# Regrouping the cross-attention rounds of a decoder layer by the shape in which TensorE's array is used

## The reference

```python
q = (layer_norm(latents) @ Wq)   # 16 heads of 64
k, v = split(layer_norm(context) @ Wkv)
k = apply_rope(k, cos, sin)
attn = softmax(clip(q k^T * 64**-0.5, -11, 11))
out = (attn v) @ Wo + bo         # added to x
```

## Time and profile before

| | |
|---|---|
| time, median of 3 runs | 442.52 us (440.68 to 444.0) |
| the profiled execution's own time | 440.72 us |
| its span, first to last instruction | 438.6 us |
| PE busy, share of the span | 413.8 us, 94% |
| PE weight loads | 306.8 us, 70% |
| DVE, POOL, ACT busy | 323.6, 258.2, 194.7 us |
| first scores of round 0, of round 30 | 60.83, 283.40 us |

### The profile page before, as it was taken

How to read it: one execution, slowest core, us unless ns; L and a number is a source line. 1 busy time by engine, 2 the same in 40 slices (tenths; PEclk the granted TensorE clock), 3 DMA queues, 4 the chain that set the end, 5 groups by cost and what they waited for, 6 DMA issues and landing times.

```text
span 438.6 us, 8443 instructions
## 1 busy us (share of the span) xinstructions
PE 413.8 (94%) x3157; PEld 306.8 (70%) x3157; DVE 323.6 (74%) x686; ACT 194.7 (44%) x310; POOL 258.2 (59%) x228
## 2 busy tenths in 40 slices
PE   3997899999999999999999999999998999999996
PEld 2666666766667766667775676768876788888884
DVE  8798758978778857986776798798676972755554
ACT  6758463746364435463544644443547453000000
POOL 6847438998778878797779674686634581000000
PEclk9999999999999999999999999999999999999999
DMA  7676405000000000000000000335627670000000
GB/s 182 175 174 93 87 11 94 0 1 0 1 2 0 1 2 0 1 1 0 2 2 0 2 1 0 147 55 81 145 36 201 116 140 1 6 6 13 6 6 13
DMA packets 75433, 19.83 MB, mean 45 GB/s; under 512 B 66741, under 2 KB 73834, under 8 KB 75394
## 3 DMA queue, kind: packets, MB, share of 16 engines
q1 hardware_dynamic: 72628, 18.27, 19.7%
q10 hardware_dynamic: 2766, 1.04, 1.0%
HBM read 17.27 MB, written 2.02 MB: 44 GB/s over the span
## 4 chain that ended last, share of the span: by engine, by line
PE 71%; DVE 12%; issue 6%; ACT 4%; POOL 3%; DMA 2%; ACTq 1%; DVEq 0%; POOLq 0%
PE psum L1191 11%; PE psum L1174 11%; PE psum L984 9%; PE psum L1365 5%; PE psum L1366 5%; PE psum L1367 5%; PE psum L1210 3%; PE psum L1332 3%; PE psum L1334 3%; PE psum L1333 3%; PE psum L1201 3%; PE psum L1093 3%; POOL xeT_lo L583 2%; DVE rden L1591 1%; ACT e_sb L811 1%
## 5 line engine op out<-in xcount | busy, mean ns | idle before, releaser
L543 POOL TENSOR_TENSOR e_part<-e_sb 128x512 f32<-128x512 f32 x64 | 89.0, 1409 | 29.7 <-DVE e_sb L1584 29.7
L811 ACT ACTIVATE e_sb<-psum 128x1024 f32<-128x1024 f32 x64 | 62.2, 1022 | 16.2 <-PE psum L1174 16.2
L1174 PE MATMUL psum<-q_t,kT 64*128 64x256 f32 x512 | 64.2, 390 | 0.0
L1191 PE MATMUL psum<-e_sb,v_sb 128*64 128x256 f32 x512 | 63.4, 386 | 0.0
L1791 DVE SCALAR_TENSOR_TENSOR x_sb<-psum,dw,x_sb 128x128 f32<-128x128 f32 x96 | 33.7, 351 | 35.8 <-PE psum L1367 33.2
L1591 DVE RECIPROCAL rden<-psum 128x256 f32<-128x256 f32 x32 | 55.8, 1745 | 0.2 <-PE psum L1201 0.2
L790 ACT ACTIVATE kT<-psum 128x512 f32<-128x512 f32 x32 | 19.1, 597 | 78.2 <-PE psum L1093 77.9
L1174 PEld LDWEIGHTS psum<-q_t,kT 64*128 64x128 f32 x512 | 46.8, 187 | 9.5 <-issue 5.0
L1584 DVE TENSOR_SCALAR e_sb<-e_sb 128x1024 f32<-128x1024 f32 x64 | 50.5, 824 | 3.8 <-ACT e_sb L811 3.8
L535 POOL TENSOR_TENSOR k_rot<-rope_a,rope_b 128x512 f32<-128x512 f32 x32 | 41.8, 1309 | 12.8 <-DVE rope_b L1471 12.8
L1191 PEld LDWEIGHTS psum<-e_sb,v_sb 128*64 128x64 f32 x512 | 33.5, 136 | 21.5 <-issue 5.8
(11 more groups left out here) (193 smaller groups left out, 764.9 us busy)
## 6 DMA issues: line engine op xcount, KB each, us to landing
w_raw<-in_L_ffn_W_dram SPq DMA_DIRECT2D x96, 64.0 KB, 2.3
gates<-gate_dram SPq DMA_DIRECT2D x6, 768.0 KB, 4.4
ctx_sb<-in_ctx_dram SPq DMA_DIRECT2D x4, 256.0 KB, 6.0
vbd<-v_dram SPq DMA_DIRECT2D x16, 52.6 KB
v_dram<-v_tok SPq DMA_DIRECT2D x4, 136.0 KB, 3.0
raw<-in_L_xattn_Wkv_dram SPq DMA_DIRECT2D x2, 256.0 KB, 5.1
k_rot<-in_L_xattn_Wkv_dram SPq DMA_DIRECT2D x2, 256.0 KB, 4.5
k_rot<-in_L_xattn_Wq_dram SPq DMA_DIRECT2D x2, 256.0 KB, 5.5
```

The source lines that it names most:

```text
L543: pool.tensor_tensor(e_part[:, p % 2, half, :, :], e_sb[:, i % ERING, :, 0, :], e_sb[:, i % ERING, :, 1, :], ALU.add)\
L811: act.activation(e_sb[:, i % ERING, :, :, :].rearrange("p a k t -> p (a k t)"), psum[:, a:a + 2, :].rearrange("p a b -> p (a b)"), ACT.Exp ...
L1174: mm = pe.matmul(psum[:, 2 * (i % 2) + a, t * S:(t + 1) * S], kT[rows, p % 3, kt * P:(kt + 1) * P], q_t[rows, j % 2, p % 2, :], start=True ...
L1191: mm = pe.matmul(psum[DX * a:DX * a + DX, pv_bank(p), 0:S], v_sb[g % 2][:, kt, 2 * pp + a, :], e_sb[:, i % ERING, a, t, :], start=(kt == 0 ...
```

## The change

Four things are done in the rounds, and one ahead of them:

- PE's order in a round becomes: scores, then everything on the whole array (extras, routing stage, value unit, queries, key unit, key transposes), then both value calls and the sums. ACT's and DVE's order follows; DVE divides at the end of a round instead of at the start of the next.
- Values and sums of all pairs use bank 4. The values of pair p wait until pair p - 1 is divided.
- Key units use bank 7, value units bank 5, and the routing stages bank 7. The routing stages stay in rounds 22 to 28, one a round.
- In bank 6 the extras now come before the queries. The key unit of before the rounds (unit 10) is rotated in round 0, behind that round's clips.
- At the start, PE multiplies the identity by itself: 11 times before the weights are there, 4 times before the first x tile, and half as wide between x tiles.

The core of the diff:

```diff
+        WARM_BANK = 4
-        UNIT_BANK = [7, 6, 7, 6, 7, 6, 7, 6, 7, 7, 5]
+        UNIT_BANK = [7, 6, 7, 6, 7, 6, 7, 6, 7, 7, 7]
-        UNIT_BANK += [5] * (len(UNIT) - len(UNIT_BANK))
+        UNIT_BANK += [5 if kind == "v" else 7 for kind, n in UNIT[len(UNIT_BANK):]]
...
+            if r in extras:
+                MISC.append(extras[r])
             if r % 2 == 0 and r // 2 + 1 < NQ:
                 MISC.append(("queries", r // 2 + 1))
-            if r in extras:
-                MISC.append(extras[r])
...
-        def pv_bank(p):
-            return 4 if p % 2 == 0 else 7
+        PV_BANK = 4
-        ROUTE = {"weights": 2 * NORM_ROUND, "tokens": 2 * NORM_ROUND + 2, "address": 2 * NORM_ROUND + 4, "scores": 2 * NORM_ROUND + 6,
-                 "chosen": 2 * NORM_ROUND + 8, "softmax": 2 * NORM_ROUND + 10, "turn": 2 * NORM_ROUND + 12}
+        ROUTE = {stage: NORM_ROUND + i for i, stage in enumerate(("weights", "tokens", "address", "scores", "chosen", "softmax", "turn"))}
+        ROUTE_BANK = 7
...
 POOL
-            key_sum(K_LEAD - 1)
             for r in range(NPAIR):
...
+                if r == 0:
+                    key_sum(K_LEAD - 1)
                 if r in ROUND_KEYS:
...
 ACT
                 if r in CONTEXT_NORM:
                     context_normalize(CONTEXT_NORM[r])
+                if r in extras and extras[r][0] == "latents":
+                    misc_wait(extras[r])
+                    latents_f(extras[r][1])
+                route_1(r)
                 if r in ROUND_VALUES:
                     value_unit(ROUND_VALUES[r])
                 if r % 2 == 0 and r // 2 + 1 < NQ:
                     queries_out(r // 2 + 1)
-                route_1(2 * r)
                 if r == NORM_ROUND:
                     final_normalize(0)
...
                 if r + 3 < NPAIR:
                     keys_turned(r + 3)
-                route_1(2 * r + 1)
...
 PE
+            def warm(times, n):
+                for _ in range(times):
+                    pe.matmul(psum[:, WARM_BANK, 0:n], ident[:, :], ident[:, 0:n], start=True, stop=True)
             pe.wait_ge(s["chain_pool"], 2)
+            warm(11, P)
             pe.wait_ge(s["ld_aw"], 80)
...
+            warm(4, P)
             for i in range(NT):
...
                 if i % 4 == 3:
                     mm.then_inc(s["xT_ps"], 1)
+                else:
+                    warm(1, P // 2)
...
 weigh_values
-                if half == 0 and p >= 2:
-                    pe.wait_ge(s["ox_done"], p - 1)
+                if half == 0 and p:
+                    pe.wait_ge(s["ox_done"], p)
...
 route_1
-                    pe.wait_ge(s["v_done"], min(i // 2 + V_LEAD, NG * KC - 1) + 1)
+                    pe.wait_ge(s["rope_done"], min(i - 1 + K_LEAD, NG * KC - 1) + 1)
...
-                if r in ROUND_VALUES:
-                    route_read(2 * r - 2)
-                    unit(ROUND_VALUES[r])
-                if r % 2 == 0 and r // 2 + 1 < NQ:
-                    queries(r // 2 + 1)
-                weigh_values(2 * r)
-                route_1(2 * r)
-                weigh_values(2 * r + 1)
-                if r < NPAIR - 1:
-                    sum_weights(r)
                 if r in extras:
...
+                route_1(r)
+                if r in ROUND_VALUES:
+                    unit(ROUND_VALUES[r])
+                if r % 2 == 0 and r // 2 + 1 < NQ:
+                    queries(r // 2 + 1)
                 if r in ROUND_KEYS:
-                    route_read(2 * r)
+                    route_read(r)
                     unit(ROUND_KEYS[r])
                 if r + 3 < NPAIR:
                     turn_keys(r + 3)
-                route_1(2 * r + 1)
+                weigh_values(2 * r)
+                weigh_values(2 * r + 1)
+                if r < NPAIR - 1:
+                    sum_weights(r)
...
 DVE
-            key_unit(10)
...
             for r in range(NPAIR):
-                if r:
-                    divide(r - 1)
...
+                if r == 0:
+                    key_unit(10)
...
-                route_1(2 * r)
                 if r in extras:
...
+                route_1(r)
                 if r in ROUND_KEYS:
                     key_unit(ROUND_KEYS[r])
-                route_1(2 * r + 1)
+                if r < NPAIR - 1:
+                    divide(r)
                 if r == NPAIR - 3:
                     dve.wait_ge(s["misc_ps"], MISC_NO["keys", NPAIR - 1] + 1)
                     expert_tokens(0)
```

More of the change, by code:

```diff
@@ L879, in route_1 @@
                     act.wait_ge(s["rt_ps"], 1)
-                    act.activation(uT[:, :], psum[0:DADDR, 5, P:P + NR * NE], ACT.Copy).then_inc(s["rt_done"], 1)
+                    act.activation(uT[:, :], psum[0:DADDR, ROUTE_BANK, P:P + NR * NE], ACT.Copy).then_inc(s["rt_done"], 1)
                 for stage in ROUTE:
                     if ROUTE[stage] == i:
-                        route(0, stage, 5)
+                        route(0, stage, ROUTE_BANK)
             for r in range(NPAIR):
@@ L897, in _ @@
                     queries_out(r // 2 + 1)
-                route_1(2 * r)
                 if r == NORM_ROUND:
                     final_normalize(0)
-                if r in extras and extras[r][0] == "latents":
-                    misc_wait(extras[r])
-                    latents_f(extras[r][1])
                 if r + 3 < NPAIR:
                     keys_turned(r + 3)
-                route_1(2 * r + 1)
                 if r == NPAIR - 3:
@@ L1183, in weigh_values @@
                 pe.wait_ge(s["v_done"], KC * (g + 1))
-                if half == 0 and p >= 2:
-                    pe.wait_ge(s["ox_done"], p - 1)
+                if half == 0 and p:
+                    pe.wait_ge(s["ox_done"], p)
                 elif half == 0:
-                    pe.wait_ge(s["oT_done"], NCH - 1 + p)
+                    pe.wait_ge(s["oT_done"], NCH - 1)
                 for t in range(KH):
@@ L1190, in weigh_values @@
                     for a in range(2):
-                        mm = pe.matmul(psum[DX * a:DX * a + DX, pv_bank(p), 0:S], v_sb[g % 2][:, kt, 2 * pp + a, :],
+                        mm = pe.matmul(psum[DX * a:DX * a + DX, PV_BANK, 0:S], v_sb[g % 2][:, kt, 2 * pp + a, :],
                                        e_sb[:, i % ERING, a, t, :], start=(kt == 0), stop=(kt == KC - 1))
@@ L1200, in sum_weights @@
                 for a in range(2):
-                    mm = pe.matmul(psum[DX * a:DX * a + DX, pv_bank(p), S:2 * S], ones[:, :], e_part[:, p % 2, 0, a, :],
+                    mm = pe.matmul(psum[DX * a:DX * a + DX, PV_BANK, S:2 * S], ones[:, :], e_part[:, p % 2, 0, a, :],
                                    start=True, stop=True)
@@ L1277, in route_1 @@
                     pe.wait_ge(s["ld_u"], 48)
-                    pe.transpose(psum[0:DADDR, 5, P:P + NR * NE], u_sb[:, :], ident[0:NR * NE, 0:NR * NE]).then_inc(s["rt_ps"], 1)
+                    pe.transpose(psum[0:DADDR, ROUTE_BANK, P:P + NR * NE], u_sb[:, :], ident[0:NR * NE, 0:NR * NE]).then_inc(s["rt_ps"], 1)
                 if i == ROUTE["tokens"]:
@@ L1590, in divide @@
                     dve.wait_ge(s["ox_done"], p - 1)
-                dve.reciprocal(rden[:, p % 2, :], psum[:, pv_bank(p), S:2 * S]).then_inc(s["rden_done"], 1)
+                dve.reciprocal(rden[:, p % 2, :], psum[:, PV_BANK, S:2 * S]).then_inc(s["rden_done"], 1)
                 dve.wait_ge(s["rden_done"], p + 1)
@@ L1594, in divide @@
                     dve.wait_ge(s["misc_ps"], MISC_NO["project", b - 2, TPB - 1] + 1)
-                dve.tensor_tensor(o_t[:, b % 2, hp, :], psum[:, pv_bank(p), 0:S], rden[:, p % 2, :], ALU.mult).then_inc(s["ox_done"], 1)
+                dve.tensor_tensor(o_t[:, b % 2, hp, :], psum[:, PV_BANK, 0:S], rden[:, p % 2, :], ALU.mult).then_inc(s["ox_done"], 1)
             def add_projected(what):
```

## The result

The kernel after takes 450.21 us (median of four runs, 449.58 to 451.11) against 442.24 us for the kernel before on the same chip: ratio 1.0196, 95% interval 1.0171 to 1.022. The forecast was 444.0, with a range up to 450; the result lies above both. The profiled execution, the lowest of the four, took 449.58 us, with a span of 447.4 us, 8.9 us more than the span before. Measured by the first scores of each round and the first expert product, the stretches share it out as follows; the last column puts the forecast's terms on the same stretches.

A forecast was written before the change was run, and what follows sets the result against it. TensorE (PE) was taken to bound the rounds, busy 217.73 of 222.60 us. The terms -7.8 - 1.6 - 2.3 + 5.4 + 3.8 + 4.0 gave +1.5 on the median 442.52, so 444.0 us, range 436 to 450.

The forecast's parts named there:

- Fewer changes of shape: Rounds: 40 fewer switches of PE's array shape between product groups, at 0.195 us each, -7.8 us.
- free: Rival, rounds: the new switch from columns to row halves costs nothing, 438.3 us; chance 0.10.
- double: Rival, rounds: the new switch from columns to row halves costs twice the others' price, 449.7 us; chance 0.07.
- Waits that come: Rounds: PE waits for ScalarE to empty the bank shared by projections, queries and keys, +5.4 us, bounds +3 to +7.
- Waits that go: Rounds 0, 13, 18, 23 and 27: PE's waits for rope products, a value copy and projected rows shrink or vanish, -2.3 us.
- Round 28: Last key transposes wait for the queries' copy, now behind ScalarE's routing step: 3.2 to 4.2 us, taken as +3.8.
- the rival on the clock: Rival, start: the clock does not rise or falls back during the transposes, no early gain, 445.6 us; chance 0.14.
- The end of the rounds: Round 30 to first expert product: division ahead of expert tokens delays the chain by +3.4 to +4.4, taken as +4.0 us.
- Start: Before the rounds: identity products raise PE's clock, first keys come at 13.2 us, -1.6 us, bounds 0 and -1.7.
- The expert stage has its own pace: Rival, experts: transposed weights or tokens set their pace, absorbing the 3.8 and 4.0 us, 436.2 us; chance 0.15.
- VectorE becomes the bound: Rival, rounds: VectorE needs 7.1 us a round as clips meet GpSimd's adds, +8, so 452 us; chance 0.14.

The follow-up runs named there:

- E8: Kernel after, with query products and their ScalarE copies ahead of the value unit in even rounds without context or latents: 449.28 us, ratio 1.0191.
- E2: Kernel after, with 20 identity products on TensorE during its wait in round 28, ScalarE's order unchanged: 447.59 us, ratio 1.0145.
- E4: Kernel after, with VectorE dividing pairs 29 and 30 behind tokens and weights, and the last pair's values and sums in bank 7: 446.19 us, ratio 1.0105.
- E10: Kernel after with E1's edit, plus a bank of its own for the last pair's values and sums: 445.15 us, ratio 1.007.
- E11: Kernel after with E1's edit, plus VectorE dividing pairs 29 and 30 behind token blocks and weights: 446.84 us, ratio 1.0111.
- E1: Kernel after, with ScalarE's copy of the queries ahead of the router's part in round 28: 446.05 us, ratio 1.0094.
- E9: Kernel before, with ScalarE doing the router's last stage ahead of the copy of the queries in round 28: 443.48 us, ratio 1.0043.
- E3: Kernel after, with the context's normalization moved behind the copy of the queries in rounds 2 and 8: 447.35 us, ratio 1.0127.

## Why the prediction was wrong

**Fewer changes of shape: right.** A plain odd round of the kernel after, PE in order of time:

```profile
98.76 2.00 PE L1180 MATMUL psum<-q_t,kT 64*128 64x256 f32 x16
100.68 0.50 PE L990 MATMUL psum<-wkv_hi,ctx_hi 128*128 128x512 f32 x1
101.02 0.39 PE L990 MATMUL psum<-wkv_lo,ctx_hi 128*128 128x512 f32 x1
...
105.01 0.49 PE L1180 MATMUL psum<-q_t,kT 64*128 64x256 f32 x2
```

98.76 to 105.01 is 6.25 us for the 6.49 of the earlier trace rows, 0.24 less where 0.195 was forecast. So the new change, from columns to row halves, costs about what the others do (0.15 us by this round), and the rivals "free" and "double" fall.

**Waits that come: the step that failed in the rounds.** It had +5.4 us with bounds of 3 and 7, and it is about 9.7: rounds 0 to 27 and 29 changed by +0.94 in all, to which the 37 lost changes outside round 28 contributed -7.2 (37 x 0.195) and the waits that went about -1.6 (below). The two large waits were right, 1.5 us in rounds 2 and 8 each; PE in round 2:

```profile
80.20 0.39 PE L990 MATMUL psum<-wkv_hi,ctx_lo 128*128 128x512 f32 x1
82.05 0.63 PE L1099 MATMUL psum<-ident,k_rot 128*128 128x128 f32 x4 [1.46 <-ACT q_t L801]
```

The profile counts the 1.46 from the end of the last product (80.59). But without a wait the transposes would have started 0.24 behind its start, at 80.44, so the wait cost 1.61, 0.15 more than its listed length.

What failed were the many small ones. "In a plain even round the copy ends without the normalization at some 4.1: cost 0.05" priced ten rounds at next to nothing, and the sum doesn't even hold that (3.0 + 0.8 + 0.6 + 1.0 is 5.4 already). Round 10 of the kernel after shows the cost, first ScalarE, then PE:

```profile
137.72 0.61 ACT L716 ACTIVATE v_sb<-psum 128x512 f32<-128x512 f32 x1
138.36 0.60 ACT L801 ACTIVATE q_t<-psum 128x512 f32<-128x512 f32 x1
```

```profile
138.04 0.28 PE L1115 MATMUL psum<-lat_hi,wq_lo 128*128 128x256 f32 x1
138.16 0.40 PE L990 MATMUL psum<-wkv_hi,ctx_hi 128*128 128x512 f32 x1
138.40 0.40 PE L990 MATMUL psum<-wkv_lo,ctx_hi 128*128 128x512 f32 x1
138.63 0.40 PE L990 MATMUL psum<-wkv_hi,ctx_lo 128*128 128x512 f32 x1
139.10 0.63 PE L1099 MATMUL psum<-ident,k_rot 128*128 128x128 f32 x4
```

The copy starts when the last query product is out and ends 0.6 us later, 4.25 us into the round, and the key unit covers only 0.7 of that way. Without a wait the transposes would start 0.24 us behind the key unit, 4.16 into the round, where the forecast had PE (4.15). But the copy ended 0.15 later than the forecast's 4.1, and the transposes started another 0.14 us after its end, a step that the forecast left out (round 28 has it too, 277.76 to 277.90). So the step from the key unit to the transposes is 0.47 instead of 0.24, and the list of waits leaves it out: counted from the end of the last product it is 0.07 us (139.03 to 139.10). It is 0.47 or 0.48 in each of the ten even rounds from 4 to 24 without 8: 2.4 us for nothing in the sum. The change of shape saves 0.195, and the round got longer, 7.18 to 7.25. E8 shows that the order is the cause: 6.97 with the queries ahead. Other rounds did the rest. Round 11 grew by 0.76 (its keys wait 0.8 us for the projected rows, which VectorE adds late). Rounds 0, 1, 12 and 26 grew by 2.1 together, where 0.6 was forecast: 0.6 and 0.8 for rounds 12 and 26, less 0.195 in each of the four (the 0.24 of round 12 is in both counts). Rounds 0 and 1 have a new wait of 0.26 us each, for ScalarE's ctx_f and for GpSimd's k_rot, which the forecast did not have.

**Waits that go: too large.** -2.3 forecast, about -1.6 measured: 0.27 in round 13, 0.46 in round 18 and 0.9 in round 27, each being what the round lost beyond its change of shape (and, in round 18, beyond the new 0.24). Round 23 was to lose 0.7, but its key unit waits 1.1 us for the copy of the transposed tokens (L990 on xnT in the list above), as much as the tokens waited before. Round 0 kept its wait for the rope products nearly whole (1.0 in that list, 1.1 in the earlier trace rows) and got the new one beside it.

**Round 28: the wait right, its sequel missing.** The chain through ScalarE was forecast at 7.4 us from the first score, and the copy ended at 277.76 (277.16 + 0.60), 7.4 us after 270.36. So the chain was right. The value taken, 3.8, lies under the 4.28 measured because the slower clip came again, which VectorE's row in that round shows:

```profile
273.52 1.67 DVE L1588 TENSOR_SCALAR e_sb<-e_sb 128x1024 f32<-128x1024 f32 x1 [0.22 <-ACT e_sb L809]
```

The larger part of the miss is the slow stretch, 1.67 us (E2), and this is the step that failed here: no term of the forecast gave a wait a price beyond its own length, and the rival on the clock looked at the start alone.

**The end of the rounds: right, a little less.** +4.0 forecast with a low end of 3.4, and 3.4 measured. PE of the kernel after:

```profile
288.91 2.00 PE L1180 MATMUL psum<-q_t,kT 64*128 64x256 f32 x16
291.99 0.47 PE L1246 MATMUL psum<-dw1T,spread 128*128 128x512 f32 x1 [1.08 <-DVE xeT L1635]
...
297.33 1.95 PE L1197 MATMUL psum<-e_sb,v_sb 128*64 128x256 f32 x16 [2.56 <-DVE o_t L1599]
299.34 0.47 PE L1246 MATMUL psum<-dw1T,spread 128*128 128x512 f32 x1
```

The spread product waits until 3.1 us after the scores (3.0 forecast), and the last values start at 8.4 (8.4 to 9.4 forecast). E4, E10 and E11 confirm the chain edit by edit.

**Start: right as far as it can be told.** The weight loads of the first queries and keys are 0.43 us apart from the second on, for 0.86 in the earlier trace rows, and VectorE has the first keys at 13.39 instead of 14.87, 1.5 us earlier (13.2 and 1.6 forecast):

```profile
11.90 0.19 PEld L961 LDWEIGHTS psum<-xT,awT 128*128 128x128 f32 x1 [0.24 <-issue]
12.33 0.19 PEld L961 LDWEIGHTS psum<-xT,awT 128*128 128x128 f32 x1 [0.24 <-issue]
...
13.39 4.18 DVE L1484 TENSOR_SCALAR kM<-psum,mask 128x512 f32<-128x512 f32 x4 [0.89 <-PE psum L961]
```

**The rivals.** "The expert stage has its own pace" falls: 147.77 us for 147.78, and the late start came through in full. "VectorE becomes the bound" falls as well. VectorE is busier in the rounds, 179.66 us from 60.0 to 277.9 where the earlier trace rows has 174.57 in a longer stretch, and its clips take 0.94 us on average for 0.82. But values wait for a division once, at the end. Against the span the sum missed by 7.4 us: 5.0 in the rounds 0 to 27, 2.5 in round 28, 0.5 at the start, and 0.6 the other way in the tail.

## What to carry to other kernels

When work is regrouped around a shared bank, price every round by the time between one user's last product and the next user's first, less the copy between them; a shortfall of 0.24 us, too short for the list of waits, ate the gain of the regrouping in every round that had it. A wait of PE costs more than its length when the clock falls behind it (1.67 us more in round 28). So the first cure is the order on the engine that empties the bank, and a cure that leaves another such wait can see the fall charged there instead (E1). Where two waits hang on one chain, as in the tail, remove them together: alone, each only moved.

## What the runs showed of the hardware

PE's granted clock fell to 0.50 behind waits of 4.28 us (the kernel after), 2.57 (E1), 2.85 (E10) and 4.25 (E11), and stayed at 1.00 behind one of 2.56 in the tail of the kernel after and one of 1.89 in E9's profiled execution. So the length of the wait alone doesn't decide: nearly the same wait in the tail was followed by a fall in E1, where round 28 had none, and by none in the kernel after. Nor does an earlier fall rule out a second one: E8 has one in round 28 and one in the tail. What decides is not settled by these runs.

A fall cost 1.67 us in round 28 (E2) and 1.6 in E1's tail and experts. Where it came inside the wait, round 28 was longer, 12.58 us in E3 and 12.64 in E4 for 12.09. Dead products through the wait of round 28 prevented the fall there, and it came in the tail instead (E2).

Only one execution of each kernel was profiled, and others of the same kernel had another mean granted clock. In six executions of E1 it lay between 0.990 and 0.999, and the one at 0.999 took 443.81 us, close to the 444 that the theory expected without a fall. In E9 three of ten, at 0.994 to 0.996, took 444.5 to 445.5 us, the other seven 441.6 to 444.1: behind 1.89 us, too, a fall may come in some executions, which no profile here shows.
